# Routing stages of two mixture-of-experts layers without their unread TensorE products

## The chip, the cores and the metric

The kernel runs on one core of one Trainium2 chip. The metric is device time in microseconds (us), the median of several runs. Where the profile speaks of a granted clock, 1.00 is TensorE at 2.4 GHz and 0.50 is TensorE at 1.2 GHz.

## What is computed

Two layers, one after the other, on 3327 nodes with 256 features (padded to 3328, which is 26 tiles of 128). Each layer is an attention over a sparse adjacency matrix and then a mixture of 8 experts, of which every node uses its best two. Each half starts with a layer norm, and its result is added to x:

```python
x = x + _L0_gnn_ref(_layernorm(x), adj, L0_gnn_W, L0_gnn_r)
x = x + _L0_ffn_ref(_layernorm(x)[None], gate_w, gate_b, W1, b1, W2, b2)[0]
x = x + _L1_gnn_ref(_layernorm(x), adj, ...)
x = x + _L1_ffn_ref(_layernorm(x)[None], Wr, br, ln_g, ln_b, W1, b1, W2, b2)[0]
```

The part that matters here is the gate of the two expert halves: `logits = x @ gate + bias` with 8 columns, the best two experts of each node with their softmax weights, and from these the list of which node goes to which expert.

## The kernel before, in words

Everything runs in float32 unless said otherwise. x lives in SBUF as `X`, 26 tiles of 128 nodes. Each layer has three stages: attention, routing, and expert tiles. The last stage runs over 59 slot tiles (`RUN_TILES`) of 128 gathered nodes, each with one expert: two transposes, 8 or 16 pairs of up products, Gelu on ScalarE, down products, and an indirect DMA that adds the rows to their total.

The change touches the routing stage alone, `route_tensor` of class `Experts`, which runs once per layer: from about 424 to 486 us, and from about 1312 to 1376 us. There is no scheduler: each engine has its own program, in the order in which it is written, and they meet on semaphores. TensorE's program in this stage is:

1. For each of 26 tiles, `turn(t)`: two 128 by 128 transposes of the tile into a bank (L2080), then `logits_of(t - 1)`: the two gate products of the tile before it, 8 columns each (L2088), and behind them two **unread products** (L2095), bfloat16 with 256 columns into bank 6, which nothing reads. A transpose waits for `xt_ready`, that is for ScalarE to have copied the turned tile two before it into `xt` (L2043); a gate product waits for the copy of its own tile.
2. 48 unread products, the wait for `picked`, and the two count products (L2104, L2105, 208 columns).
3. 96 unread products, a product of zeros that opens bank 5 (L2108), and four groups of 13 slot products (L2114). Each product of float32 leaves two records in the trace, so a group has 26 and a tile's gate products have four; the transposes have one record each. Group c waits for `hot_ids` and `hot_w`, and at its end it raises `hot_used[c % 2]`.

ScalarE (`route_scalar`) copies the turned tiles in pairs. Behind the fifth pair it runs the layer norm's square root (`layer_norm_sqrt`, L2334), which waits for the variances from VectorE and has an activation table load ahead of it; in layer 1 a second square root (L2053) stands behind the seventh pair. In layer 0 a last Gelu of the attention stands behind the second pair. Later it multiplies the hot tiles by the weights (L2066).

VectorE (`route_vector`) computes the layer norm statistics, waits for ScalarE's square root, scales all 26 tiles of `X` in place in 13 rounds of two (L1923, each waits for `tp_ready`, the tile's transpose), waits for all 26 `lg_done`, and then runs one long chain of small steps: the first and second choice (L1936 to L1953), which raises `picked`; after `cnt_done` the prefix sums and the places (L1955 to L1980); and then four groups of hot tiles (L2017, L2022, L2026). Groups 2 and 3 reuse the buffers of groups 0 and 1 and wait for `hot_used`. At the end it writes `slot_row`, for which the gathers of the next stage wait on GpSimd's queue.

The sync engine's queue stores the scaled `X` to DRAM in two halves, behind `x_scaled`, and loads the second weight matrix around it.

Of the kernel before, what the change touches and what calls it, by code (L numbers as in the profile page):

```python
# [31 lines left out]
BF16 = mybir.dt.bfloat16  # L32
# [8 lines left out]
P = 128  # L41
# [53 lines left out]
def program(nc, x_in, adjT, w0T, w0, r0, w1, w1T, uv1, proj_wT, bias1, proj_b1,  # L95
# [3 lines left out]
    with ctx:  # L99
        def sb(name, shape, dt=F32):  # L100
            return ctx.enter_context(nc.sbuf_tensor(name, shape, dt))
# [7 lines left out]
        def hand_over():  # L109
            got, ones_ = list(held), list(start_at_one)  # L110
            held.clear()
            start_at_one.clear()
            return got, ones_

        bank = [ctx.enter_context(nc.psum_tensor(f"bank{i}", [P, 512], F32)) for i in range(8)]
# [10 lines left out]
        ident = sb("ident", [P, P])  # L126
# [19 lines left out]
        ones = sb("ones", [P, P], BF16)  # L146
# [1572 lines left out]
        class Experts:  # L1719
# [352 lines left out]
            def route_tensor(self, pe, rows):  # L2072
                def turn(t):

                    i, s = t // 2, t % 2
                    if s == 0:
                        pe.wait_ge(*rows(i))
                    pe.wait_ge(self.xt_ready[s], i + 1)
                    for k in range(KC):
                        last = pe.transpose(bank[self.turn_banks[s]][:, k * P:(k + 1) * P],  # L2080
                                            X[:, t * D + k * P:t * D + (k + 1) * P], ident[:, :])
                    last.then_inc(self.tp_ready[s], 1)

                def logits_of(t):
                    i, s = t // 2, t % 2
                    pe.wait_ge(self.xt_ready[s], i + 2)
                    for k in range(KC):
                        last = pe.matmul(bank[2][:, t * E:(t + 1) * E], self.xt[s][:, k * P:(k + 1) * P],  # L2088
                                         gate[:, k * E:(k + 1) * E], start=(k == 0), stop=(k == KC - 1))
                    last.then_inc(self.lg_done, 1)  # L2090
                    idle_products(2)

                def idle_products(n):
                    for _ in range(n):
                        pe.matmul(bank[6][:, 0:2 * P], ones[:, :], ident[:, :].bitcast(BF16), start=True, stop=True)  # L2095

                turn(0)
                for t in range(1, T):
                    turn(t)
                    logits_of(t - 1)  # L2100
                logits_of(T - 1)
                idle_products(48)
                pe.wait_ge(self.picked, 3)
                pe.matmul(bank[3][:, 0:T * E], earlier[:, :], self.routed, start=True, stop=True)  # L2104
                pe.matmul(bank[4][:, 0:T * E], ones[:, :], self.routed, start=True, stop=True  # L2105
                          ).then_inc(self.cnt_done, 1)
                idle_products(96)
                pe.matmul(bank[5][:, 0:2 * SLOT_TILES], zeros[:, 0:P], zeros[:, 0:2 * SLOT_TILES],  # L2108
                          start=True, stop=True)
                for c in range(4):  # L2110
                    pe.wait_ge(self.hot_ids[c % 2], c // 2 + 1)
                    pe.wait_ge(self.hot_w[c % 2], c // 2 + 1)
                    for q in range(PAIRS):
                        last = pe.matmul(bank[5][:, 0:2 * SLOT_TILES],  # L2114
                                         self.hot_place[c % 2][:, q * P:(q + 1) * P],
                                         self.hot_tile[c % 2][:, q * 2 * SLOT_TILES:(q + 1) * 2 * SLOT_TILES],
                                         start=False, stop=False, skip_group_check=True)
                    last.then_inc(self.hot_used[c % 2], 1)
# [217 lines left out]
        first_sems, _ = hand_over()  # L2336
# [228 lines left out]
```

## Time and profile before

| | us |
|---|---|
| runs | 1820.1, 1821.03, 1821.04 |
| median of the runs | 1821.03 |
| span of the profiled execution | 1815.9 |
| median of the runs less that span | 5.1 |
| TensorE busy in the span | 1664.2 (92%) |
| VectorE busy | 929.7 (51%) |
| ScalarE busy | 953.4 (53%) |
| unread products (L2095), busy, 392 of them | 53.1 |
| gate products (L2088), busy, 208 records | 27.1 |
| mean granted clock of TensorE | 0.973 |

The profiled execution has no device time of its own beside its span; what lies around the span is the 5.1 us of the table. Times inside the profile are counted from the start of the span. A busy time is a sum over instructions, and one record of a product lasts longer than the distance from its start to the next start, since products overlap; where a cost per product is wanted, the distance of starts is the thing to read.

### The profile page before, as it was taken

What the parts mean: (1) busy time and instruction counts of PE and PEld (TensorE: products, weight loads), DVE (VectorE), ACT (ScalarE), POOL (GpSimd) and SP (SyncE); (2) the same over time, 40 slices, a digit from 0 to 9 for tenths busy, and PEclk for the clock granted to TensorE, in tenths of its full rate; (3) what the DMA queues carried; (4) which work ended last, traced back from release to release, by engine and by line L of the source; (5) the groups of instructions that cost most, each with busy time, mean ns of one, the idle gap of its engine ahead of it and who ended that gap; (6) DMA issues with size and microseconds to landing.
All of it is one profiled execution on the core that took longest, in us unless ns stands there. A gap on an engine that the chain in (4) does not pass through costs nothing.

```text
span 1815.9 us, 41552 instructions
## 1 busy us (share of the span) xinstructions
PE 1664.2 (92%) x13344; PEld 1538.0 (85%) x13345; DVE 929.7 (51%) x2185; ACT 953.4 (53%) x2191; POOL 351.2 (19%) x315
## 2 busy tenths in 40 slices
PE   4799999999799997778989989989988999999998
PEld 3588788778799996657989989989987999999997
DVE  4578868788522221548878868867771111111111
ACT  1133444444333333467989979889834344434433
POOL 2110000000166665310000000000002333333332
PEclk9899999999899998889999999999999999999999
DMA  9990000104388886400000000000185666666664
GB/s 160 107 170 10 9 10 9 38 18 165 123 208 208 208 208 155 150 15 13 14 13 18 9 19 13 9 19 17 46 295 189 174 180 186 181 176 181 190 176 96
DMA packets 85580, 189.95 MB, mean 105 GB/s; under 512 B 13209, under 2 KB 59545, under 8 KB 76665
## 3 DMA queue, kind: packets, MB, share of 16 engines
q1 hardware_dynamic: 53177, 139.39, 23.3%
q0 software_dynamic: 31504, 48.97, 17.3%
q8 instruction: 46, 0.75, 0.2%
q10 hardware_dynamic: 816, 0.53, 0.1%
q14 instruction: 37, 0.30, 0.1%
HBM read 188.98 MB, written 33.11 MB: 122 GB/s over the span
## 4 chain that ended last, share of the span: by engine, by line
PE 51%; DVE 4%; issue 2%; ACT 1%; DMA 1%; DVEq 0%; POOL 0%; ACTq 0%; POOLq 0%
PE bank L1703 23%; PE bank L2187 12%; PE bank L2226 11%; PE bank L663 1%; PE bank L666 1%; PE bank L2194 1%; ACT arena L1427 1%; DMA arena<-qd 1%; DVE arena L1546 0%; DVE arena L1548 0%; PE bank L2088 0%; DVE arena L1464 0%; PE bank L653 0%; DVE X L2022 0%; DVE arena L1470 0%
## 5 line engine op out<-in xcount | busy, mean ns | idle before, releaser
L1703 PE MATMUL bank<-arena 128*128 128x195 bf16 x5408 | 473.6, 249 | 38.3 <-DVE arena L1548 20.2
L1703 PEld LDWEIGHTS bank<-arena 128*128 128x128 fp8e4 x5408 | 468.8, 98 | 43.0 <-issue 41.4
L1427 ACT ACTIVATE arena<-arena,m_row 128x512 fp8e5<-128x512 f32 (+1 forms) x672 | 402.4, 678 | 70.9 <-DVE arena L1548 48.2
L2187 PEld LDWEIGHTS bank<-X,arena 128*128 128x128 f32 x2832 | 335.7, 193 | 10.0 <-issue 3.7
L2187 PE MATMUL bank<-X,arena 128*128 128x128 f32 x2832 | 338.8, 277 | 0.3
L2290 DVE TENSOR_TENSOR arena<-bank,X 128x256 f32<-128x256 f32 x118 | 50.1, 425 | 563.3 <-PE bank L2226 514.3
L1274 PE MATMUL bank<-arena 128*128 (+1 forms) x1352 | 312.5, 386 | 17.3 <-DVE arena L1180 15.0
L2226 PE MATMUL bank<-arena,X 128*128 x1416 | 325.0, 379 | 1.4 <-ACT X L2264 1.4
L1274 PEld LDWEIGHTS bank<-arena 128*128 128x128 f32 x1352 | 252.5, 191 | 58.5 <-issue 23.7
L2226 PEld LDWEIGHTS bank<-arena,X 128*128 128x128 f32 x1416 | 259.9, 190 | 32.4 <-issue 1.9
L1132 ACT ACTIVATE bank<-arena,s_all 128x384 f32<-128x384 f32 (+1 forms) x234 | 133.7, 573 | 187.6 <-DVE arena L1172 183.6
L2264 ACT ACTIVATE X<-bank,arena 128x128 f32<-128x128 f32 x708 | 195.4, 378 | 63.8 <-issue 56.9
L1172 DVE SCALAR_TENSOR_TENSOR arena<-arena,d_all,bank 128x384 f32<-128x384 f32 (+1 forms) x234 | 138.7, 593 | 69.6 <-PE bank L1274 59.4
L2246 ACT ACTIVATE X<-bank,arena 128x128 f32<-128x128 f32 x118 | 47.5, 453 | 232.3 <-PE bank L2194 232.3
L2122 POOL IOTA arena<- 128x128 f32 x2 | 0.5, 238 | 836.9 <-DVEq L1605 522.3
L1546 DVE SCALAR_TENSOR_TENSOR arena<-arena 128x512 uint32<-128x512 uint32 (+1 forms) x168 | 109.4, 651 | 90.6 <-PE bank L1703 69.4
L2175 POOL DMA_INDIRECT out<-X,slot_row x59 | 93.1, 1577 | 269.5 <-DVE X L2293 266.5
L2157 POOL DMA_INDIRECT arena<-xs,slot_row x118 | 116.3, 986 | 146.1 <-DVE slot_w L2037 110.8
L1180 DVE TENSOR_TENSOR arena<-arena 128x384 f32<-128x384 f32 (+1 forms) x234 | 124.8, 536 | 0.0
L1548 DVE SCALAR_TENSOR_TENSOR arena<-arena 128x512 uint32<-128x512 uint32 (+1 forms) x168 | 108.6, 646 | 0.0
L2242 ACT COPY X<-bank 128x256 f32<-128x256 f32 x59 | 22.0, 372 | 103.6 <-PE bank L2194 101.5
L2194 PE MATMUL bank<-ident,arena 128*128 128x128 f32 x236 | 46.1, 278 | 11.1 <-DMA arena<-xs,slot_row 8.7
(240 smaller groups left out, 1336.7 us busy)
## 6 DMA issues: line engine op xcount, KB each, us to landing
arena<-m1w SPq DMA_DIRECT2D x67, 1024.0 KB, 10.8
arena<-m0w SPq DMA_DIRECT2D x67, 512.0 KB
xs<-X SPq DMA_DIRECT2D x4, 1664.0 KB, 6.8
arena<-qd SPq DMA_DIRECT2D x25, 256.0 KB, 3.2
arena<-adjT POOLq DMA_DIRECT2D x13, 448.0 KB, 12.7
arena<-adjT POOLq DMA_DIRECT2D x13, 384.0 KB, 10.8
xe<-zeros POOLq DMA_DIRECT2D x1, 3456.0 KB, 22.0
X<-x_in SPq DMA_DIRECT2D x2, 1664.0 KB, 11.4
```

What stands on the lines that cost most here:

```text
L1132: a.activation(self.exp_bank[s][:, 0:nt * P], self.rows[r][:, 0:nt * P], ACT.Exp, bias=s_all[:, at(c, 1)]).then_inc(self.exp_ready[s], 1)
L1172: v.scalar_tensor_tensor(out=self.prob[q][:, 0:w], in0=self.rows[r][:, W:W + w], scalar=d_all[:, at(c, 1)], in1=self.exp_bank[s][:, 0:w], ...
L1180: v.tensor_tensor(self.prob[q][:, 0:w], self.prob[q][:, 0:w], mask[:, at(c * NP + b * W, w)], ALU.min).then_inc(self.prob_ready[q], 1)
L1274: last = pe.matmul(bank[3 * r + n][:, 0:D + 1], self.prob[q][:, n * P:(n + 1) * P], V[:, at(c * VW, D + 1)], start=False, stop=False, skip ...
L1427: last = a.activation(self.sign[slot].bitcast(F8W)[:, q * W:q * W + nt * P], self.row[r][:, 0:nt * P], ACT.Sigmoid, scale=STEEP, bias=self ...
L1546: v.scalar_tensor_tensor(out=pos, in0=sg, scalar=1, in1=m, op0=ALU.logical_shift_left, op1=ALU.bitwise_and).then_inc(self.pos_ready, 1)
L1548: v.scalar_tensor_tensor(out=neg, in0=sg, scalar=0x08080808, in1=m, op0=ALU.bitwise_xor, op1=ALU.bitwise_and).then_inc(self.neg_ready[slot ...
L1703: last = pe.matmul(bank[rb * NT + n][:, kind * KW:(kind + 1) * KW], self.split[slot][kind].bitcast(F8)[:, q * W + n * P:q * W + (n + 1) * ...
L2157: pool.indirect_dma_start(self.rx[g % 4], None, xs[:, :], bass.IndirectOffsetOnAxis(ap=slot_row[:, g:g + 1], axis=0)).then_inc(self.rx_loa ...
L2187: last = pe.matmul(bank[2 * s + c // 4][:, c % 4 * P:(c % 4 + 1) * P], self.W1[s][:, k * HID + c * P:k * HID + (c + 1) * P], self.rxt[s][: ...
L2226: last = pe.matmul(bank[5 + s][:, 0:D], self.ht[s][:, c * P:(c + 1) * P], self.W2[:, at(e * (HC * D) + c * D, D)], start=(c == 0), stop=(c ...
L2264: last = a.activation(self.ht[s][:, c * P:(c + 1) * P], bank[2 * s + c // 4][:, c % 4 * P:(c % 4 + 1) * P], ACT.Gelu, bias=self.b1[:, at(e ...
```

## The change

All unread products of the routing stage go: the two behind each tile's gate products, the 48 behind the last gate product, and the 96 behind the counts, in both layers. The helper that issued them goes too. Nothing is moved, no wait is added or taken away, and nothing read them.

```diff
                     last.then_inc(self.lg_done, 1)
-                    idle_products(2)
-
-                def idle_products(n):
-                    for _ in range(n):
-                        pe.matmul(bank[6][:, 0:2 * P], ones[:, :], ident[:, :].bitcast(BF16), start=True, stop=True)
 
                 turn(0)
                 for t in range(1, T):
                     turn(t)
                     logits_of(t - 1)
                 logits_of(T - 1)
-                idle_products(48)
                 pe.wait_ge(self.picked, 3)
                 pe.matmul(bank[3][:, 0:T * E], earlier[:, :], self.routed, start=True, stop=True)
                 pe.matmul(bank[4][:, 0:T * E], ones[:, :], self.routed, start=True, stop=True
                           ).then_inc(self.cnt_done, 1)
-                idle_products(96)
                 pe.matmul(bank[5][:, 0:2 * SLOT_TILES], zeros[:, 0:P], zeros[:, 0:2 * SLOT_TILES],
                           start=True, stop=True)
```

The lines below `route_tensor` move up by seven, and so L2104 becomes L2098, L2105 becomes L2099, L2108 becomes L2101 and L2114 becomes L2107.

TensorE's instructions at the start of the routing stage of layer 0, before (L2080 the transposes of tiles of `X`, L2088 the gate products, whose gate lies in `slot_w` and whose turned tile `xt` in the arena, L2095 the unread ones):

```order
L2080 MATMUL bank<-ident,X 128x128 x4
L2088 MATMUL bank<-slot_w,arena 128x8 x2
L2095 MATMUL bank<-ident,ones 128x256 x2
L2080 MATMUL bank<-ident,X 128x128 x2
L2088 MATMUL bank<-slot_w,arena 128x8 x2
L2095 MATMUL bank<-ident,ones 128x256 x2
```

and in the changed kernel:

```order
L2080 MATMUL bank<-ident,X 128x128 x4
L2088 MATMUL bank<-slot_w,arena 128x8 x2
L2080 MATMUL bank<-ident,X 128x128 x2
L2088 MATMUL bank<-slot_w,arena 128x8 x2
L2080 MATMUL bank<-ident,X 128x128 x2
L2088 MATMUL bank<-slot_w,arena 128x8 x2
```

The transposes of a tile now stand directly behind the gate products of the tile before the last. The end of the gate products and the counts of layer 0, before:

```order
L2088 MATMUL bank<-slot_w,arena 128x8 x2
L2095 MATMUL bank<-ident,ones 128x256 x50
L2104 MATMUL bank<-arena,earlier 128x208
L2105 MATMUL bank<-arena,ones 128x208
L2095 MATMUL bank<-ident,ones 128x256 x96
L2108 MATMUL bank<-zeros 128x118
L2114 MATMUL bank<-X 128x118 x52
```

and in the changed kernel:

```order
L2088 MATMUL bank<-slot_w,arena 128x8 x4
L2098 MATMUL bank<-arena,earlier 128x208
L2099 MATMUL bank<-arena,ones 128x208
L2101 MATMUL bank<-zeros 128x118
L2107 MATMUL bank<-X 128x118 x52
```

Between the last gate product and the last slot product only the two counts and the product of zeros are left.

## Rows read from the trace of the kernel before

**Rows 1.** The page: the chain that ended last, by line.

```profile
PE bank L1703 23%; PE bank L2187 12%; PE bank L2226 11%; PE bank L663 1%; PE bank L666 1%; PE bank L2194 1%; ACT arena L1427 1%; DMA arena<-qd 1%; DVE arena L1546 0%; DVE arena L1548 0%; PE bank L2088 0%; DVE arena L1464 0%; PE bank L653 0%; DVE X L2022 0%; DVE arena L1470 0%
```

**Rows 2.** Timeline of TensorE, layer 0 (start, length, engine, line, tiles, shape, count).

```profile
425.37 0.38 PE L2080 MATMUL bank<-ident,X 128*128 128x128 f32 x2
425.59 0.51 PE L2088 MATMUL bank<-slot_w,arena 128*128 128x8 f32 x4
425.95 0.38 PE L2095 MATMUL bank<-ident,ones 128*128 128x256 bf16 x2
426.17 0.38 PE L2080 MATMUL bank<-ident,X 128*128 128x128 f32 x2
```

**Rows 3.** Timeline of ScalarE, layer 0: copies, table load, square root.

```profile
425.79 0.37 ACT L2043 COPY arena<-bank 128x256 f32<-128x256 f32 x1 [0.88 <-PE bank L2080]
...
431.39 0.37 ACT L2043 COPY arena<-bank 128x256 f32<-128x256 f32 x1 [0.43 <-PE bank L2080]
431.78 1.28 ACT L2334 ACT_TABLE_LOAD   x1
433.07 0.23 ACT L2334 ACTIVATE rstd<-rstd 128x26 f32<-128x26 f32 x1
```

**Rows 4.** Timeline of VectorE, layer 0: variance, scaling, selection, third group.

```profile
432.52 0.18 DVE L2326 TENSOR_SCALAR rstd<-mv 128x26 f32<-128x26 f32 x1
...
434.44 0.74 DVE L1923 TENSOR_SCALAR X<-X,arena  x2 [0.49 <-DVE arena L1913]
...
446.29 0.37 DVE L1936 TENSOR_TENSOR arena<-bank,rstd 128x208 f32<-128x208 f32 x1
...
470.36 0.96 DVE L2017 TENSOR_TENSOR arena<-tile_no,arena 128x767 f32<-128x767 f32 x1 [0.34 <-PE bank L2114]
```

**Rows 5.** Timeline of TensorE, layer 0: behind the square root, counts, slot products.

```profile
433.61 0.61 PE L2088 MATMUL bank<-slot_w,arena 128*128 128x8 f32 x4 [0.66 <-ACT arena L2043]
...
452.69 0.26 PE L2104 MATMUL bank<-arena,earlier 128*128 128x208 bf16 x1 [1.06 <-DVE arena L1953]
...
465.56 7.67 PE L2114 MATMUL bank<-X 128*128 128x118 f32 x52 [1.99 <-ACT X L2066]
```

**Rows 6.** Windows of 3 to 4.5 us: busy time by engine, granted clock, DMA.

```profile
463.50:466.50 3.00, 1.01 (x10) 0.97 (x9) 3.00 (x4) 2.68 (x13) 0.00 (x0) 1.00 0.01 3
466.60:469.90 3.30, 3.30 (x18) 3.30 (x17) 3.20 (x6) 2.29 (x10) 0.00 (x0) 0.50 0.00 0
...
726.50:731.00 4.50, 4.41 (x20) 4.34 (x20) 0.00 (x1) 0.00 (x0) 3.24 (x4) 0.50 0.98 334
...
1319.90:1323.30 3.40, 2.74 (x27) 2.47 (x26) 0.87 (x4) 2.26 (x5) 0.00 (x0) 1.00 1.03 310
```

**Rows 7.** Timeline of TensorE between the layers: 8-column products at half clock.

```profile
726.97 1.00 PE L572 MATMUL bank<-arena 128*128 128x8 f32 x4
727.82 0.57 PE L570 MATMUL bank<-arena,ident 128*128 128x8 f32 x2
```

**Rows 8.** Timeline of ScalarE, layer 1: tenth copy and both square roots.

```profile
1319.35 0.37 ACT L2043 COPY arena<-bank 128x256 f32<-128x256 f32 x1 [0.43 <-PE bank L2080]
...
1321.04 0.23 ACT L2334 ACTIVATE rstd<-rstd 128x26 f32<-128x26 f32 x1
...
1323.74 0.23 ACT L2053 ACTIVATE arena<-arena 128x26 f32<-128x26 f32 x1
```

**Rows 9.** Timeline of VectorE, layer 1: reciprocal, selection, third group.

```profile
1321.30 0.32 DVE L2328 RECIPROCAL rstd<-rstd 128x26 f32<-128x26 f32 x1 [4.03 <-ACT rstd L2334]
...
1337.13 0.37 DVE L1936 TENSOR_TENSOR arena<-bank,rstd 128x208 f32<-128x208 f32 x1
...
1360.60 0.94 DVE L2017 TENSOR_TENSOR arena<-tile_no,arena 128x767 f32<-128x767 f32 x1
```

**Rows 10.** Timeline of TensorE, layer 1: first and third group of slot products.

```profile
1356.22 3.13 PE L2114 MATMUL bank<-X 128*128 128x118 f32 x26
...
1364.87 3.13 PE L2114 MATMUL bank<-X 128*128 128x118 f32 x26 [2.05 <-ACT X L2066]
```

## Prediction

> **What bounds the kernel now.** I read first the page's chain that ended last. Its largest line is an attention product [rows 1], and no unread product is among the lines it prints, so only a stage in which TensorE's pace or clock matters can carry the result. That is the routing stage, once per layer. I read it on the timelines of TensorE, ScalarE and VectorE, and its granted clock in windows.
>
> Gate products, layer 0. A tile costs TensorE 0.80 us: two transposes 0.22 (425.37 to 425.59), four records of gate products 0.36 (to 425.95), two unread products 0.22 (to 426.17) [rows 2]. But VectorE sets the end of this part. It needs the layer norm's square root, then scales X in 13 rounds, and only then does the selection start, at 446.29 [rows 4]. The square root stands on ScalarE behind the tenth copy (431.39) and a table load of 1.28 us, at 433.07 [rows 3]; the variance was ready at 432.52 + 0.18 = 432.70 [rows 4]. The scaling starts 1.37 us behind the square root and takes 11.85 us up to the selection [rows 3, 4]. TensorE's last gate product, 16 tiles behind the square root, is done just before that too. Layer 1 is the same but for its order: the variance is ready early and VectorE waits 4.03 us for the square root [rows 9], which ScalarE reaches at 1321.04; a second one follows at 1323.74 [rows 8]; the selection starts at 1337.13 [rows 9].
>
> Behind the gate products VectorE's chain of small steps is the path. TensorE waits for it before the counts (idle 1.06 us) and for ScalarE before the first slot group (idle 1.99 us) [rows 5].
>
> **The change, part by part.**
>
> The 48 and the 96 unread products lie beside VectorE's chain. Gone, they give nothing: the counts already waited [rows 5], and the first slot group of layer 1 ran at 1356.22, right behind the 96 [rows 10], 0.1 to 0.2 us at most after its weights were there. I count zero.
>
> The two per tile give TensorE 0.22 us, but not all of it. From the start of a turn to its copy on ScalarE passes 0.42 us (425.37 to 425.79) [rows 2, 3], and as much again from the copy's start to the gate product that it frees; I take 0.42, an estimate from the square root at 433.07, which with one copy behind it frees the product at 433.61, 0.54 later [rows 3, 5]. So two tiles take 0.42 + 0.42 + 0.36 = 1.20, and one 0.60. ScalarE reaches its square root earlier: one gap of 0.22 and seven of 0.20, 1.6 us. In layer 1 all of that is a gain, 1321.04 becomes 1319.4. In layer 0 ScalarE then waits for the variance at 432.70, so the square root comes at 432.76, 0.31 earlier.
>
> This opens a hole on TensorE that was not there. In layer 0 it has turned all it can at about 431.0 and goes on at 432.76 + 0.54 = 433.3: 2.3 us without a product. In layer 1 the hole is 1.2 us (1318.7 to 1319.95), where it was 0.66. And what stands before and behind the hole is thinner: half of a tile's time went to 256-column products.
>
> The clock is what decides. Before, the whole part runs at 1.00, with a hole of 0.66 us in it (the window from 1319.9) [rows 6]. Later in layer 0 TensorE is idle for 1.99 us before the first slot group [rows 5], and just behind that it runs at 0.50 for 3.3 us [rows 6]. A hole of 2.3 us among thinner work should do the same in layer 0: I take the clock as half when TensorE resumes at 433.3. Layer 1 is less sure: a hole of 2.05 us before its third slot group [rows 10] is followed by a group at full speed (3.13 us, as the first), but that one lies among dense products of 118 columns.
>
> Does it come back while gate products run? The only rows with products of 8 columns back to back without filler are those between the layers: four records cost 0.85 us there (726.97 to 727.82) [rows 7], and over 4.5 us with TensorE busy for 4.41 the clock stays at 0.50 [rows 6]. The transposes between them are what no row shows alone. I take it that the clock stays half to the end of the gate products, as in the row nearest to them. A tile then costs 0.85 and twice the transposes' 0.22, 0.43: 1.28 us.
>
> Sum, half clock in both layers:
> - Layer 0: from 433.30, gate products of tile 10 (0.85), 14 rounds of 1.28 (17.9), tile 25 (0.85), 0.15 to land: 453.05, against the selection at 446.29: **+6.8**.
> - Layer 1: from 1319.4 + 0.54 = 1319.95, the same 19.75: 1339.7 against 1337.13: **+2.6**.
> - Counts: 0.26 us for the first [rows 5]; at half clock both together take 0 to 0.3 more; I take +0.2 in each layer, nearer the doubled end, since their hole is now over 5 us.
> - First slot group: it starts after many us without a product. At full clock 26 records take 3.13 [rows 10], at half about 18 per 3.3 us [rows 6], so 4.8, or 4.4 if the clock returns on the way. VectorE's third group waits for it. In layer 0 this group was already slow (465.56 to 470.36) [rows 4, 5], so -0.3 to +0.4, taken as +0.2. In layer 1 VectorE came at 1360.60 [rows 9], 4.4 us after the start: 0 to +0.7, taken as +0.5.
>
> Together 7.2 + 3.3 = 10.5 us on the profiled execution's span of 1815.9, whose surroundings bring it to 1821.0, the median: **1831.5 us**. Later half-clock stretches, behind the first gathers and in layer 1's attention, begin at another moment; they move either way by about 1 us.
>
> The stores of X and the second half of the weights, which SP issues behind the scaling, move later with it by up to 7 us. They are wanted some 40 us later (first down products), so I count zero; without that cover it would be their full delay.
>
> **The rivals.**
>
> *The clock holds, or comes back soon, 0.28.* Not slower. In layer 0 the selection then comes 0.3 earlier and the tail costs 0.4; in layer 1 the scaling starts 2.2 earlier (1.6 for the first square root, three tiles less 0.2 for the second) or, with some half-clock tiles between, 0.8, and the tail costs 0.7. Sum 0.1 - 1.5 to 0.1 - 0.1, so -1.4 to 0: about 1820.3 us. The point from which it decides: TensorE may run at half for n of the last 16 tiles of layer 0 as long as 16 x 0.60 + 0.68 n stays under 12.5 us, so n up to 4, some 5.5 us. For it: TensorE is busy without a hole through these tiles, and the half-clock stretch before the slot groups ended after 3.3 us of work [rows 6]. Against: that work had 118 columns, and 4.4 busy us of 8 columns did not do it. The Trainium skill ("TensorE: Matmul & The Clock Gate", Part 1) has the clock return after sustained activity, which by TensorE's busy time gives this rival; the window from 726.5 disagrees as far as busy time is meant.
>
> *Layer 1 keeps its clock, 0.12.* Its hole is short. Then layer 1 gives -1.5 in place of +3.3 (-2.2 for the scaling, +0.7 for the tail): 7.2 - 1.5 = 5.7, 1826.7 us.
>
> *The clock falls at once, 0.12.* Without the 256-column products transposes and 8 columns are not enough, and the first ten tiles slow down too. Some three tiles more at 1.28 before layer 1's square root: 3 x 0.68 = 2.0, less little; in layer 0 most of it hides behind the variance, 0.2. Sum about 12.5, 1833.5 us. The same page (Part 4) says that transposes do not count as busy for the clock; then this rival is the likely one. The window from 1319.9, full clock with a hole of 0.66 us, speaks mildly against.
>
> That the change does not do what it says is out: both order pieces show the products gone.
>
> **How the numbers follow.** Both layers at half clock 0.48, layer 1 spared 0.12, falling at once 0.12, clock kept or regained 0.28. A measurement of this kernel can tell 0.2%, 3.6 us, from no change. The first three are all above it: slower 0.72. Of the last nearly all lies within: same 0.26; faster by 3.6 us would need both layers' gains whole and a better phase of the later stretches, 0.02. The forecast is the likeliest, 1831.5. The range has to take in the fourth case, since it alone is more than 2 in 10: from 1819.6 (-1.4) to 1834.6 (12.5 and 1 us of phase). The slower cases alone would have 1826 to 1834.6.
>
> **What the profile would show.** Right: granted clock 0.50 from about 432.5 to the end of the gate products of layer 0, gate products there 1.28 us per tile, and L1923 paced by transposes, 2.5 us per round; selection at about 453 (layer 0), and 2 to 3 us late in layer 1 after that shift. ScalarE's copies 0.60 apart before the square root. Wrong: clock back to 1.00 within 5 us of 433 and the selection at 446; or copies slower than 0.8 apart before the square root, which is the third rival.

## The result and the profile after

The changed kernel takes 1826.13 us (median of 5 runs, 1825.44 to 1827.41), the kernel before in the same group 1820.21 us (5 runs, 1818.37 to 1821.04). The ratio is 1.0042, with a 95% interval of 1.0031 to 1.0053: it is slower, by 5.9 us between the medians and 7.6 us by the ratio. In a second group of runs it was 1827.27 against 1818.38, ratio 1.0051 (1.0038 to 1.0064), 8.9 us between the medians. The forecast was 1831.5, +10.5 us.

The page of the changed kernel; the last line is the clock granted in 40 equal slices, in tenths:

```profile
span 1823.7 us, 40768 instructions
...
PE 1648.1 (90%) x12952; PEld 1527.6 (84%) x12953; DVE 929.9 (51%) x2185; ACT 954.5 (52%) x2191; POOL 351.5 (19%) x315
...
PEclk9899999996799999889999999999959999999999
```

The unread products were busy for 53.1 us, and yet TensorE is busy only 16 us less. The granted clock shows a 6 and a 7 (tenth and eleventh slice) where the routing stage of layer 0 lies, for a 9 and an 8 on the page before, and a 5 for a 9 in layer 1. The groups of TensorE's instructions by line, in the columns of the page (busy us, mean ns of one, idle before it):

```profile
L2088 PE MATMUL bank<-slot_w,arena 128*128 128x8 f32 x208 | 42.1, 314 | 0.5 <-ACT arena L2043 0.5
L2080 PE MATMUL bank<-ident,X 128*128 128x128 f32 x104 | 30.8, 397 | 0.0
```

Before, the gate products were busy for 27.1 us at 239 ns each; now the same 208 records take 42.1. The timeline of TensorE in layer 0:

```profile
423.93 0.51 PE L2088 MATMUL bank<-slot_w,arena 128*128 128x8 f32 x4
424.29 0.41 PE L2080 MATMUL bank<-ident,X 128*128 128x128 f32 x2
424.55 0.61 PE L2088 MATMUL bank<-slot_w,arena 128*128 128x8 f32 x4
425.02 0.41 PE L2080 MATMUL bank<-ident,X 128*128 128x128 f32 x2
...
427.12 0.86 PE L2088 MATMUL bank<-slot_w,arena 128*128 128x8 f32 x4
427.84 0.67 PE L2080 MATMUL bank<-ident,X 128*128 128x128 f32 x2
428.30 0.86 PE L2088 MATMUL bank<-slot_w,arena 128*128 128x8 f32 x4
...
449.70 1.71 PE L2088 MATMUL bank<-slot_w,arena 128*128 128x8 f32 x8
457.85 0.36 PE L2098 MATMUL bank<-arena,earlier 128*128 128x208 bf16 x1 [6.44 <-DVE arena L1953]
...
470.88 7.51 PE L2107 MATMUL bank<-X 128*128 128x118 f32 x52 [12.40 <-ACT X L2066]
```

The first tiles follow each other at 0.61 and 0.73 us in turn (423.68, 424.29, 425.02, 425.64). Three tiles later a tile takes 1.17 us: 0.46 from the transposes to the gate products (427.84 to 428.30) and 0.71 back. It stays at 1.17 to the last gate product, but for one tile beside the square root (1.45). The windows show why. Their columns are the stretch, its length, the busy time of each engine with its count, the granted clock, the DMA share and GB/s:

```profile
422.30:426.10 3.80, 3.56 (x32) 3.08 (x30) 3.52 (x10) 2.19 (x7) 0.00 (x0) 1.00 0.16 56
426.30:451.30 25.00, 25.00 (x127) 24.69 (x126) 15.28 (x47) 9.98 (x24) 0.23 (x1) 0.50 0.53 184
...
1315.50:1320.40 4.90, 4.66 (x43) 4.17 (x41) 4.27 (x17) 2.52 (x7) 0.24 (x1) 1.00 1.04 346
1320.60:1343.40 22.80, 22.80 (x116) 22.49 (x115) 11.50 (x35) 9.49 (x23) 0.00 (x0) 0.50 0.87 321
1363.00:1368.20 5.20, 5.20 (x25) 5.20 (x26) 4.17 (x6) 3.15 (x13) 0.00 (x0) 0.50 0.00 0
```

In layer 0 the clock is at 1.00 for the first 3.8 us of gate products and at 0.50 for the 25 us behind them, with TensorE busy for all of those 25 us, so there is no hole in them. Layer 1 is the same, 4.9 and 22.8 us. The square root on ScalarE, layer 0:

```profile
430.89 0.37 ACT L2043 COPY arena<-bank 128x256 f32<-128x256 f32 x1 [0.80 <-PE bank L2080]
431.28 1.28 ACT L2327 ACT_TABLE_LOAD   x1
432.57 0.23 ACT L2327 ACTIVATE rstd<-rstd 128x26 f32<-128x26 f32 x1
```

It stands at 432.57, 10.24 us behind the stage's first transpose (422.33). Before, it was 9.26 behind it (433.07 less 423.81) [rows 3]. VectorE in layer 0:

```profile
431.04 0.18 DVE L2319 TENSOR_SCALAR rstd<-mv 128x26 f32<-128x26 f32 x1
432.83 0.32 DVE L2321 RECIPROCAL rstd<-rstd 128x26 f32<-128x26 f32 x1 [1.61 <-ACT rstd L2327]
...
443.16 0.41 DVE L1923 TENSOR_SCALAR X<-X,arena  x1 [0.40 <-PE bank L2080]
...
451.45 0.37 DVE L1936 TENSOR_TENSOR arena<-bank,rstd 128x208 f32<-128x208 f32 x1 [0.84 <-PE bank L2088]
...
475.52 0.96 DVE L2017 TENSOR_TENSOR arena<-tile_no,arena 128x767 f32<-128x767 f32 x1 [0.19 <-PE bank L2107]
```

The variance is ready at 431.22, and now VectorE waits 1.61 us for the square root. The scaling catches up with TensorE at 443.16 and then waits for each transpose; the selection waits 0.84 us for the last gate product and starts at 451.45, 29.12 us behind the first transpose, where it was 22.48 [rows 4]. VectorE in layer 1:

```profile
1324.94 0.32 DVE L2321 RECIPROCAL rstd<-rstd 128x26 f32<-128x26 f32 x1 [4.02 <-ACT rstd L2327]
...
1329.76 0.74 DVE L1923 TENSOR_SCALAR X<-X,arena  x2 [0.50 <-DVE arena L1913]
...
1343.56 0.38 DVE L1936 TENSOR_TENSOR arena<-bank,rstd 128x208 f32<-128x208 f32 x1 [0.84 <-PE bank L2088]
...
1368.58 0.96 DVE L2017 TENSOR_TENSOR arena<-tile_no,arena 128x767 f32<-128x767 f32 x1 [1.31 <-PE bank L2107]
```

The selection starts 28.10 us behind the first transpose (1315.46), where it was 25.32 [rows 9], and the third group waits 1.31 us for the first slot group.

The table gathers the stages of the profiled executions. Each column is worked out from two starts on the timelines: the stage's first transpose, VectorE's first step of the selection (L1936), its first step behind the counts (L1955), the third group of hot tiles, the write of `slot_w`, the first up product of the expert tiles, and TensorE's first work behind the first two tiles' up products. The last two rows are from the trace of the second group of runs, of the same changed kernel.

| us | first transpose to selection | to counts | to third group | to `slot_w` | to first up product | up products | whole |
|---|---|---|---|---|---|---|---|
| before, layer 0 | 22.48 | 6.79 | 17.28 | 11.52 | 5.79 | 4.90 | 68.76 |
| changed, layer 0 | 29.12 | 6.97 | 17.10 | 11.53 | 5.72 | 6.01 | 76.45 |
| before, layer 1 | 25.32 | 6.81 | 16.66 | 11.50 | 6.43 | 8.49 | 75.21 |
| changed, layer 1 | 28.10 | 6.99 | 18.03 | 11.53 | 6.34 | 8.24 | 79.23 |
| changed, second trace, layer 0 | 29.29 | 6.97 | 18.38 | 11.52 | 5.75 | 5.13 | 77.04 |
| changed, second trace, layer 1 | 28.25 | 6.98 | 17.77 | 11.53 | 6.42 | 9.70 | 80.65 |

The stages account for 7.7 + 4.0 = 11.7 us in the first trace and 8.3 + 5.4 = 13.7 in the second. The first spans differ by 7.8 (1823.7 less 1815.9), and the runs by 5.9 to 8.9. Of the 7.7 of layer 0, 0.9 is no loss: behind the up products TensorE waits for ScalarE's Gelu, 1.41 us before and 0.57 in the changed kernel, so its first down product comes only 6.8 later (77.40 us behind the first transpose for 70.56). The rest of the gap has a section of its own below.

### The profile page after: what moved, and what is told of

It is laid out like the page before. It is cut to its first block, busy times and chain, and to the rows that moved or that the text cites. A ratio compares the mean times of both kernels' runs of the same rounds, so it can differ in the third digit from the quotient of the medians.

```text
span 1823.7 us, 40768 instructions
## 1 busy us (share of the span) xinstructions
PE 1648.1 (90%) x12952; PEld 1527.6 (84%) x12953; DVE 929.9 (51%) x2185; ACT 954.5 (52%) x2191; POOL 351.5 (19%) x315
## 4 chain that ended last, share of the span: by engine, by line
PE 52%; DVE 4%; issue 2%; ACT 1%; DMA 1%; POOL 0%; ACTq 0%; DVEq 0%; POOLq 0%
PE bank L1703 23%; PE bank L2180 12%; PE bank L2219 11%; PE bank L663 1%; PE bank L666 1%; PE bank L2088 1%; PE bank L2187 1%; PE bank L2080 1%; DMA arena<-qd 1%; ACT arena L1427 1%; DVE arena L1548 1%; PE bank L2107 0%; DVE arena L1546 0%; DVE arena L1464 0%; ACT X L2066 0%
```

## The experiments

In all tables and texts "the 48" and "the 96" are the two rows of unread products before and behind the counts, and a "filler" is an unread product (or transpose) put in for the clock. Every timed kernel had its own runs of the kernel before in its group: 1820.86 us in the first (four kernels), 1820.42 in the second (four), 1818.38 in the third (four, one of them the changed kernel again). A difference in us is one between medians.

### Only the rows go, the products per tile stay

```diff
-                idle_products(48)
...
-                idle_products(96)
```

> The two unread products per tile stay, the 48 and the 96 go. Theory (the products per tile hold the clock, the long rows only cover waits of VectorE's chain): gate products at 1.00, selection where it was; counts 0.17 us later in each layer, the first slot group at half clock costs nothing in layer 0 and up to 1.3 us in layer 1; sum +0.3 to +1.7 us against before. Rival (the long rows carry the loss, since they hold the clock through the selection): most of the 6 us of the whole change, +4 or more.

Measured 1819.18 us, ratio 0.9997 (0.9989 to 1.0006): no difference. Windows of its trace, in the columns of the windows above:

```profile
423.80:446.20 22.40, 21.50 (x210) 20.37 (x208) 18.56 (x56) 12.08 (x30) 0.23 (x1) 1.00 0.62 216
447.40:471.00 23.60, 5.96 (x28) 5.65 (x29) 20.82 (x55) 6.81 (x28) 0.00 (x0) 0.50 0.47 161
1311.90:1337.00 25.10, 21.60 (x210) 20.37 (x208) 15.57 (x52) 12.30 (x30) 0.24 (x1) 1.00 1.00 358
```

The gate products run at 1.00 and the selection is where it was (22.47 and 25.32 us behind the first transpose). The clock is at half for 24 us behind them, all the way through VectorE's chain, and in the trace it costs 0.2 us at the counts (6.97 for 6.79) and 1.0 and 1.5 us at the third group (18.26 us in layer 0 and 18.12 in layer 1, for 17.28 and 16.66). The stages of this trace are 1.2 and 1.4 us longer than before; the runs show none of it. By the runs the rows are not where the change loses.

### Only the products per tile go

```diff
-                    idle_products(2)
```

> Only the two unread products per tile go, the 48 and the 96 stay. Theory: the clock falls to 0.50 within 4 us of the first gate product, a tile then costs 1.17 us, and the selection starts 6.6 us (layer 0) and 2.8 us (layer 1) later, counted from the first transpose of the stage; the 48 start at half clock, take about 7 us and hold the counts back by 0 to 0.5 us; sum +6 to +10 us. Rival (the long rows carry it): below +3 us.

Measured 1828.10 us, ratio 1.0043 (1.0030 to 1.0056), as much as the whole change. Half clock begins at 430.7 (6.4 us behind the first transpose) and in layer 1 at 1321.6 (4.4 us), and the selection starts 27.80 and 28.44 us behind the first transpose. So the loss of the runs comes with the products per tile. This trace also shows the clock coming back within the row of 48, which begins at half clock at 451.93:

```profile
452.00:454.50 2.50, 2.50 (x14) 1.75 (x14) 2.21 (x6) 0.28 (x1) 0.00 (x0) 0.50 0.92 310
454.70:458.00 3.30, 3.30 (x32) 2.96 (x31) 3.04 (x9) 0.00 (x0) 0.00 (x0) 1.00 1.00 274
```

### One unread product per tile

```diff
-                    idle_products(2)
+                    idle_products(1)
```

> One unread product per tile in place of two, the rest as before. If the clock holds, a tile costs 0.60 to 0.70 us at 1.00, the square root of layer 1 comes 0.8 us earlier and the selection 0.3 (layer 0) and 1.1 us (layer 1) earlier: -1.4 us. If one product is too little work for the clock, it falls as in the changed kernel and the result is +6 to +10 us. I give the first 0.6.

Measured 1828.57 us, ratio 1.0045 (1.0030 to 1.0059), but the 8 runs lie in two clumps, three from 1821.8 to 1824.4 and five from 1827.8 to 1830.8. The profiled one took 1821.86, so its trace speaks for the first clump alone; the mean granted clock of the whole run is 0.961 to 0.966 in the first and 0.958 to 0.961 in the second. Its windows, two of layer 0 and one of layer 1:

```profile
423.30:433.70 10.40, 8.95 (x86) 8.38 (x84) 9.24 (x31) 6.08 (x15) 0.23 (x1) 1.00 0.62 206
433.90:452.00 18.10, 18.10 (x99) 18.06 (x99) 9.58 (x26) 6.13 (x15) 0.00 (x0) 0.50 0.41 146
1315.60:1340.00 24.40, 23.32 (x224) 22.14 (x222) 15.86 (x53) 12.29 (x30) 0.24 (x1) 1.00 1.03 370
```

and its timeline of TensorE where the clock turns, with the like place of layer 1 in the last line:

```profile
430.66 0.51 PE L2088 MATMUL bank<-slot_w,arena 128*128 128x8 f32 x4
431.02 0.27 PE L2095 MATMUL bank<-ident,ones 128*128 128x256 bf16 x1
431.13 0.38 PE L2080 MATMUL bank<-ident,X 128*128 128x128 f32 x2
432.72 0.61 PE L2088 MATMUL bank<-slot_w,arena 128*128 128x8 f32 x4 [1.21 <-ACT arena L2043]
...
433.99 0.38 PE L2095 MATMUL bank<-ident,ones 128*128 128x256 bf16 x1
...
1324.56 0.61 PE L2088 MATMUL bank<-slot_w,arena 128*128 128x8 f32 x4 [0.84 <-ACT arena L2043]
```

Ten tiles at 1.00, then the hole at the square root, 1.21 us, and 1.1 us behind it the clock is at half until the end of the gate products. In layer 1 it held, and there the selection came 24.34 us behind the first transpose, 1.0 earlier than before, as hoped. I had given 0.6 to a clock that holds; it holds in one layer and not in the other of one and the same execution. The hole was 1.21 us where the clock fell and 0.84 where it held. That the longer hole is what made it fall fits the order in time, but no run changed the hole alone, and the second clump has no trace.

### Two unread transposes per tile in place of two products

```diff
-                    idle_products(2)
+                    for _ in range(2):
+                        pe.transpose(bank[6][:, 0:P], ident[:, :], ident[:, :])
```

> In place of the two unread products of each tile two unread transposes of 128 by 128 float32 (same 0.22 us of TensorE), the rest as before. If transposes count as work for the clock like products, nothing changes: clock 1.00, tile 0.80 us, within 1 us of before. If they do not count (Trainium skill, TensorE: Matmul & The Clock Gate, Part 4), the clock falls as in the changed kernel, a tile costs 1.6 us at half clock and layer 0's selection comes over 10 us later: +12 us or more.

Measured 1820.62 us, ratio 0.9999 (0.9987 to 1.0011). Windows of the gate products of both layers:

```profile
423.20:446.30 23.10, 22.27 (x209) 21.72 (x208) 18.66 (x56) 11.98 (x30) 0.23 (x1) 1.00 0.61 211
1314.40:1340.00 25.60, 24.77 (x233) 23.95 (x232) 15.73 (x52) 12.29 (x30) 0.24 (x1) 1.00 0.98 353
```

The clock stays at 1.00 in both, hole included, and the selection starts 23.19 and 25.68 us behind the first transpose, later than before by 0.7 and 0.4 since a tile takes 0.84 us for 0.80. So transposes hold the clock as well as products of 256 columns do. The Trainium skill ("TensorE: Matmul & The Clock Gate", Part 4) says that the full clock does not engage for transposes and that they do not count as busy in the same way. For these float32 transposes the measurement decides against it: two of them per tile held 1.00 in both layers, where without any filler the clock fell.

### The products per tile go in one layer alone

```diff
-                    idle_products(2)
+                    if self.second_norm:
+                        idle_products(2)
```

> The two unread products per tile go in layer 0 alone; 48 and 96 stay in both layers. Theory (each layer's loss is its own selection coming late): layer 0's selection +5.3 to +6.7 us after the stage's first transpose, layer 1's stage as before (selection 25.3 us after its first transpose); sum +5 to +8 us. Rival (the layers share the loss through the phase of the clock): layer 1's stage changes too, by 1 us or more.

Measured 1819.42 us, ratio 1.0001 (0.9991 to 1.0010): no difference, although its trace shows the loss. Layer 0's selection starts 27.79 us behind the first transpose (+5.3), the whole stage takes 73.95 (+5.2), and layer 1's stage is as before (75.15). Its span is 1815.9, that of the trace before to a tenth; where the loss went is followed below. The forecast of +5 to +8 us was missed.

With `if not self.second_norm:`, and so without them in layer 1:

> The same in layer 1 alone. Theory: layer 0's stage as before (selection 22.5 us after its first transpose), layer 1's selection +2.5 to +3.3 us, since there VectorE scales late anyway and hides the rest; with the tail of the 48 at half clock a little more; sum +2.5 to +4.5 us. Together with the run without them in layer 0 it should give the run without them in both (+7 us) within 2 us.

Measured 1822.08 us, ratio 1.0011 (1.0001 to 1.0021), +2.0 us by the ratio. One of its 12 runs took 6055.15 us and is left out of the ratio; the median of the other 11 is 1821.44, +1.0 us. The trace: layer 0 as before but for 1.2 us at its first expert tiles, layer 1's selection 27.41 us behind the first transpose (+2.1), the counts 1.5 us late behind the 48, which began at half clock, 1.0 more between third group and `slot_w` (12.50 for 11.50), and the whole stage 79.70 (+4.5). The stages of the traces add up to 9.7 (5.2 and 4.5), against 11.7 (6.6 and 5.2) with both layers' gone. The runs are further apart: 0 and +1 to +2 against +7.2 to 7.8. The runs in one layer missed the forecast sum by far more than the 2 us that I had allowed.

### The clock once down, and the fillers back

```diff
-                    idle_products(2)
+                    if t >= 10:
+                        idle_products(2)
...
-                idle_products(48)
...
-                idle_products(96)
```

> No unread products behind the first ten tiles, two behind each of the last 16, no 48 and no 96. If a thin stretch lets the clock fall and a filled one brings it back, it falls within 7 us of the stage's start and returns some 4 to 8 us behind the hole at the square root, so the selection is 1 to 4 us late in layer 0 and 0 to 2 in layer 1: +1 to +5 us. Rival (once fallen it stays down until a dense stretch without gaps): a tile of 1.6 us to the end, selection 10 us late or more.

Measured 1836.83 us against 1818.38, ratio 1.0107 (1.0094 to 1.0120), +18.5 us between the medians and 19.5 by the ratio. That is the rival, and twice the 8.9 us of taking everything away in the same group of runs. Windows of layer 0: before the fall, after it, and with the fillers back:

```profile
422.00:426.50 4.50, 4.25 (x38) 3.79 (x37) 4.24 (x12) 2.56 (x7) 0.00 (x0) 1.00 0.24 84
426.70:432.90 6.20, 6.20 (x32) 5.89 (x33) 4.65 (x19) 3.50 (x8) 0.23 (x1) 0.50 0.91 304
433.00:455.50 22.50, 22.50 (x120) 21.55 (x121) 10.02 (x26) 6.46 (x15) 0.00 (x0) 0.50 0.32 111
```

and the timeline of one filled tile at half clock:

```profile
433.86 0.86 PE L2088 MATMUL bank<-slot_w,arena 128*128 128x8 f32 x4
434.57 0.59 PE L2096 MATMUL bank<-ident,ones 128*128 128x256 bf16 x2
434.95 0.63 PE L2080 MATMUL bank<-ident,X 128*128 128x128 f32 x2
435.38 0.86 PE L2088 MATMUL bank<-slot_w,arena 128*128 128x8 f32 x4
```

From 433 on TensorE runs the very sequence of the kernel before (two transposes, four gate records, two unread products) without a hole. Before, that ran at 1.00 with 0.80 us per tile and even bridged a hole of 0.66 us [rows 2, 5, 6]. Here it stays at 0.50 for 22.5 us at 1.52 us per tile, and in layer 1 too (selection 33.03 us behind the first transpose). **The same stream keeps a clock that is up and does not raise one that is down.** At half clock its instructions also come at about half the rate, 1.52 us per tile for 0.80, and whether that or the state of the clock decides, these runs do not part. Before the clock rose, TensorE had run slot products back to back in the kernel before [rows 6] and in this one, and unread products back to back in the row of 48 of the run above. So fillers must be there from the first tile, or the clock must be raised again by a dense row.

### A delay without the clock

```diff
+                for _ in range(16 if not self.second_norm else 0):
+                    step(v.tensor_tensor(lg3, bank[2][:, 0:TE].rearrange("p (t e) -> p t e", e=E),
+                                         spread(rstd[:, :]), ALU.mult))
```

> The kernel before, with VectorE's first step of the selection repeated 16 times more in layer 0 (0.41 us each, 6.5 us), TensorE's program as it was: a delay of layer 0's stage that has no clock in its cause. Theory (a late routing stage passes to the end as it is): +6.5 us, less at most 1. Rival (part of it is taken back behind the stage): +1 to +4 us, and then the same holds for what the change loses in layer 0.

> The same with 32 repetitions, 13.1 us. If the stage's delay passes on whole, +13 us; if a fixed slack behind the stage takes part of it, the result stands 6.5 us over the run with 16; if a share of it is taken back, both are short by the same share.

With 16 repetitions (6.49 us in the trace) 1826.55 us, ratio 1.0054 (1.0041 to 1.0067), +8.2 between medians; with 32 repetitions 1832.51, ratio 1.0076 (1.0063 to 1.0088), +14.1. Neither is less than what was put in, 6.5 and 13.1 us. The smaller one is 1.7 us over it, and its trace shows where: from the third group to `slot_w` passes 12.50 us for 11.52, and the whole stage takes 76.75, 8.0 more than before. The larger one's takes 81.42, 12.7 more. So a late stage of layer 0 passes on whole, and the missing loss of the run without fillers in layer 0 is no general slack.

### More fillers

```diff
-                idle_products(48)
+                idle_products(84 if self.second_norm else 52)
...
-                idle_products(96)
+                idle_products(112)
...
                     last.then_inc(self.hot_used[c % 2], 1)
+                idle_products(40)
```

> More unread products in place of fewer: 52 (layer 0) and 84 (layer 1) before the counts, 112 behind them, and 40 behind the last slot product, ahead of the first expert tile; two per tile as before. Theory: TensorE stays at 1.00 from the gate products into the expert tiles, so layer 0's third group no longer waits (-0.3 us) and the first expert tile of each layer runs at full clock (-1.4 to -2 us each): -2 to -4 us. Rival (the 40 stand in the way of the first transposes of gathered rows, or the clock falls all the same while they wait): 0 to +1 us.

Measured 1816.54 us, ratio 0.9976 (0.9967 to 0.9986), -3.9 us. And with the square roots of layer 1 moved forward on ScalarE:

```diff
-                    if i == 4:
+                    if i == (3 if self.second_norm else 4):
                         layer_norm_sqrt(a, self, 1, (0, T))
-                    if i == 6 and self.second_norm:
+                    if i == 4 and self.second_norm:
```

> The last kernel's products, and in layer 1 the first square root one pair earlier and the second two pairs earlier (behind the fourth and the fifth pair of copies). Theory: in layer 1 VectorE waited 4.0 us for the first square root; it comes 1.6 us earlier, the second about 3 us, and the scaling with it; TensorE's gate products then end with the scaling, so the selection gains 2 to 3 us on top of the last kernel: -4 to -7 us in all. Rival (copies held back by the square roots put TensorE behind, so that the gate products set the selection): at most 1 us on top.

Measured 1814.82 us, ratio 0.9970 (0.9960 to 0.9980), -5.6 us: faster than both kernels of this study. ScalarE in layer 1:

```profile
1316.59 0.23 ACT L2335 ACTIVATE rstd<-rstd 128x26 f32<-128x26 f32 x1
...
1317.85 0.22 ACT L2053 ACTIVATE arena<-arena 128x26 f32<-128x26 f32 x1 [0.50 <-DVE arena L1906]
```

The first square root stands 7.63 us behind the first transpose for 9.23 before, the second 1.26 us behind it for 2.70 [rows 8], and the selection comes 22.94 us behind the first transpose, 2.4 earlier. But the 84 products now hold the counts back: from selection to counts 8.98 us for 6.81. With a shorter row there the two together should give some 2 us more; that was not tried. TensorE in layer 0 around the 40:

```profile
479.66 4.53 PE L2095 MATMUL bank<-ident,ones 128*128 128x256 bf16 x40
...
485.87 3.74 PE L2188 MATMUL bank<-X,arena 128*128 128x128 f32 x32
...
493.25 2.05 PE L2227 MATMUL bank<-arena,X 128*128 x6 [3.43 <-ACT X L2265]
```

The up products of the first two tiles take 3.57 us at full clock, 1.3 less than before, and it gains nothing: TensorE then waits 3.43 us for ScalarE's Gelu, for 1.41 before. Before, the first Gelu stood 11.2 us behind `slot_w` and in the changed kernel 11.4 (493.07 less 481.88, and 498.43 less 487.05); in the first kernel of this section it stood 12.4 behind it, with TensorE far ahead. In the code it waits for `b_loaded`, which takes in the second bias that SP loads behind the first two gathers. That this load is what it waited for I read from the program, no run changed it. In the stages of these two traces I find under 1 us of gain, where the runs show 4 to 6.

## What the stages say and what the runs say

Two baselines were mixed in the forecast. The profiled execution of the changed kernel is one of its runs, 1825.44 us with a span of 1823.7: around a span lie 1.7 us, not the 5.1 that I took from the median of other runs. The trace before, with 1815.9, is then an execution of about 1817.6 us, 3 us below the median of its kernel in the first group of the experiments (25 runs between 1817.56 and 1827.71), 2.8 and 0.8 below those of the other two. A sum made on that trace belongs on 1817.6.

That does not close the gap. The traces can be followed from end to end. The table gives, less the trace before, the start of layer 0's routing stage (before any edited instruction has run), each layer's stage up to its first down product (so with the wait for the first Gelu in it), what lies between the two, and the whole span; then the runs. Before, these are 423.81, 70.56, 817.44, 75.43 and 1815.9 us. What lies behind layer 1's first down product is the same within 0.2 us.

| us, less before | start | layer 0 | between | layer 1 | span | runs |
|---|---|---|---|---|---|---|
| the change | -1.5 | +6.8 | -1.7 | +4.0 | +7.8 | +5.9 |
| the change, second group | -1.0 | +8.2 | -3.0 | +5.4 | +9.6 | +8.9 |
| products per tile gone | +0.5 | +6.2 | -1.3 | +5.1 | +10.5 | +7.2 |
| gone in layer 0 | -1.6 | +5.8 | -4.0 | -0.1 | 0.0 | -1.0 |
| gone in layer 1 | -0.5 | +1.1 | +0.4 | +4.5 | +5.7 | +1.0 |
| late fillers | -1.8 | +12.4 | -3.4 | +9.5 | +16.7 | +18.5 |
| 16 repetitions | -1.1 | +9.0 | -0.2 | +0.1 | +7.6 | +8.2 |
| 32 repetitions | +0.8 | +14.0 | -1.4 | 0.0 | +13.4 | +14.1 |
| more fillers | -1.2 | +0.8 | +0.2 | -0.7 | -0.9 | -3.9 |

Every trace without the products per tile shows the loss in the stages. What offsets it lies outside them. The start differs by up to 2.3 us within the table between kernels that have done the same work until then, and that is scatter. The stretch between the stages is shorter where layer 0's gate products ran at half clock: 813.4 to 816.1 us (mean 814.7) in those six executions (the change twice, the products per tile gone, gone in layer 0, one per tile, late fillers), 815.7 to 819.0 in the other eight (mean 817.1), and 817.2 and 816.1 in the two with repetitions. So some 2.4 us seem to be given back behind a layer 0 that lost its clock. That is one execution each, the ranges overlap by 0.4 us, and the comparison was made after the fact. For the second group I had expected +6 to +8 us with layer 0's stage 6.5 to 7 and layer 1's 3.5 to 4.5 us longer, and as the rival that the runs stay 3 us or more below the stages. The stages came out at 8.3 and 5.4 and the runs at 8.9: the forecast was missed, and the rival holds.

How the give-back comes about, through the later stretches of half clock that begin at another moment, or through where an edit puts TensorE's code, was not tested and stays open, and so does why the runs of the kernels without them in one layer stay some 5 to 7 us below their stages. What is shown is where the change loses time and by which mechanism; its size in the runs is known only as 5.9 to 9.3 us.

## Why the prediction came out as it did

The direction and the range (1819.6 to 1834.6) were right, and the size of 10.5 us lies near the 11.7 of the stages and above the 5.9 to 9.3 of the runs. The main mechanism, half clock on the gate products, was right too. The way there was in part another one, and that the sum came so near the stages is partly luck.

- **What bounds the stage**: right. The rows of 48 and 96 counted zero, and their run shows no difference.
- **A tile at full clock, 0.60 us**: 0.61 and 0.73 in turn. Right enough, but it lasted only 3.9 us in layer 0.
- **ScalarE reaches the square root 1.6 us earlier, and a hole of 2.3 and 1.2 us opens**: this step failed. The clock had fallen before, the tenth copy came at 430.89, and the square root 10.24 us behind the first transpose, 1.0 later than before, in layer 1 9.22 for 9.23. There was no hole at all on TensorE. I had the wrong cause of the fall: "a hole of 2.3 us among thinner work". Work without fillers was enough, as the third rival had it ("the clock falls at once", 0.12). If a hole is a cause anywhere, it is with one product per tile, and there it is not shown.
- **The clock stays at half to the end of the gate products**: right in both layers, and against the rival that expected it back. The late fillers show that it is more than right: even the stream with its fillers does not bring it back.
- **A tile at half clock, 1.28 us**: 1.17. The four gate records take 0.71 and not the 0.85 of the 8-column products between the layers [rows 7], the transposes 0.46.
- **Selection +6.8 and +2.6**: +6.6 and +2.8, since more tiles at half clock at a lower price each made about the same sum. The two errors covered each other, by luck.
- **Counts +0.2 each**: +0.18 each.
- **First slot group, +0.2 and +0.5, at most 0.7**: -0.2 in layer 0 and +1.4 in layer 1. In layer 1 all its 26 records ran at 0.50, 25 per 5.2 us, 0.21 us each. I had 0.18 from a window that counts starts [rows 6], and I let the clock come back on the way, which it did only behind the group.
- **Later half-clock stretches, 1 us either way**: the up products of the first tiles took 1.1 us more in layer 0 and 0.25 less in layer 1.
- **The third rival's own sum, 1833.5**: too high by its price of a tile and by starting from 1821.0.

The chances: 0.72 on slower was right. The likeliest case had the right end state and the wrong moment; 0.12 was too little for a fall at once. I had held the window at the square root, full clock with a hole, for evidence that thinner work would do, but in that window the fillers were there.

## What to carry to other kernels

Where TensorE runs narrow products paced by another engine, a filler that costs it 0.22 us per tile can be what keeps a tile at 0.80 and not 1.17 us. Fill from the first such tile on, because a stream that holds the clock need not restore it. The rows of fillers where TensorE only waits gave nothing that the runs show (ratio 0.9997 without them); longer rows and 40 more ahead of the expert tiles gave 3.9 us, of which the traces explain under 1. And size a row of fillers by the shortest wait that it covers: 84 before the counts cost 2.2 us when the selection came earlier.

## What the runs showed of the hardware

- Held and regained are not the same: two transposes, four records of 8 columns and two products of 256 columns per 0.80 us keep the clock at 1.00 across a hole of 0.66 us, and the same stream without a hole stays at 0.50 for 22.5 us, at 1.52 us per tile.
- Unread products back to back do restore it: the row of 48 began at 0.50 at 451.93 and ran at 1.00 from 454.7 on, where the products per tile were gone.
- Without fillers the clock fell 3.9 us (layer 0) and 5.0 us (layer 1) behind the stage's first transpose in one execution of the changed kernel and 3.5 and 4.6 in another, and 6.4 and 4.4 us in another kernel with the same gate products: the moment is not fixed by the program.
- Two unread float32 transposes per tile hold the clock as well as two unread products (ratio 0.9999).
- Full busy time says nothing of the clock: 25 us with TensorE busy throughout at 0.50.
